# Last group of four tiles in an attention kernel: three of its six exponential additions move from POOL to VectorE

## What is computed

```python
def _L0_attn_ref(x, Wq, bq, Wk, bk, Wv, bv, Wo, bo):
    q = (x @ Wq + bq).reshape(B, S, H, DK)          # H = 16 heads, DK = 64
    k = x @ Wk + bk                                 # one key and one value for all heads
    v = x @ Wv + bv
    scores = jnp.einsum('bshd,btd->bhst', q, k) / np.sqrt(DK).astype(x.dtype)
    w = jax.nn.softmax(scores, axis=-1)
    out = jnp.einsum('bhst,btd->bshd', w, v).reshape(B, S, H * DV)
    return out @ Wo + bo

def _L0_ffn_ref(x, gate_w, gate_b, w1, b1, w2, b2, w3, b3):
    probs = jax.nn.softmax(logits, axis=1)          # over the tokens
    vals, idx = jax.lax.top_k(probs, 2)
    # three layers with relu for each of 8 experts, y; then
    v = jnp.einsum('ebso,bse->eo', y, w_tok)
    return jnp.einsum('bse,eo->bso', ind, v)

x = x + 0.5 * ffn(layernorm(x)); x = x + attn(layernorm(x)); x = x + 0.5 * ffn(layernorm(x))
```

## Time and profile before

| | us |
|---|---|
| median of 3 runs | 1040.29 |
| lowest and highest | 1039.52 and 1041.52 |
| the profiled execution, its device time | 1043.1 |
| its span, from the first to the last instruction | 1041.3 |

### The profile page before, as it was taken

The page is one execution under the profiler, slowest core; times in us unless marked ns, Lnnn a source line. Parts: engine busy times, 40 slices in busy tenths (PEclk is TensorE's granted clock), DMA queues, the critical chain, the costliest instruction groups (busy, mean ns, idle before and its releaser), DMA issues.

```text
span 1041.3 us, 18673 instructions
## 1 busy us (share of the span) xinstructions
PE 1008.1 (97%) x7140; PEld 660.8 (63%) x7140; DVE 767.7 (74%) x1029; ACT 619.1 (59%) x874; POOL 698.9 (67%) x367
## 2 busy tenths in 40 slices
PE   8899998899999999999999999999999998999996
PEld 6676886546657566556655665745565465876884
DVE  7989997867875676567576578556757646789996
ACT  5695565667754565456474467467746454685563
POOL 4475554766886689488498578756849757665653
PEclk9999998999999999999999999999999999999999
DMA  5720810001110100001001010012000213521612
GB/s 170 245 82 6 258 63 21 1 3 33 32 23 22 43 23 22 23 23 42 23 23 35 11 42 23 23 34 67 28 23 22 64 36 112 182 82 62 202 64 82
DMA packets 31407, 61.72 MB, mean 59 GB/s; under 512 B 10566, under 2 KB 15831, under 8 KB 31319
## 3 DMA queue, kind: packets, MB, share of 16 engines
q1 hardware_dynamic: 30096, 58.41, 18.7%
q10 hardware_dynamic: 1222, 2.12, 0.6%
HBM read 56.32 MB, written 3.67 MB: 58 GB/s over the span
## 4 chain that ended last, share of the span: by engine, by line
PE 84%; DVE 8%; issue 2%; ACT 2%; POOL 2%; DMA 1%; SPq 0%; DVEq 0%; ACTq 0%; POOLq 0%
PE ring L1047 21%; PE ring L981 6%; PE ring L1059 6%; PE ring L1005 5%; PE ring L1011 5%; PE ring L1007 5%; PE ring L1009 5%; PE ring L755 4%; PE ring L761 4%; PE ring L757 4%; PE ring L1020 3%; PE ring L778 2%; PE ring L779 2%; PE ring L781 2%; DVE ring L1606 2%
## 5 line engine op out<-in xcount | busy, mean ns | idle before, releaser
L1763 DVE TENSOR_REDUCE mx<-ring 128x2 f32<-128x1024 f32 x248 | 290.5, 1226 | 64.4 <-PE ring L981 64.3
L638 POOL TENSOR_TENSOR sum_picksT<-sum_picksT,P_wb 128x1024 f32<-128x1024 f32 x128 | 312.5, 2441 | 18.6 <-POOL sum_picksT L638 0.4
L1388 ACT ACTIVATE P_wb<-ring 128x1024 f32<-128x1024 f32 x256 | 262.3, 1027 | 54.6 <-PE ring L1011 25.2
L638 POOL TENSOR_TENSOR sum_picksT<-P_wb 128x1024 f32<-128x1024 f32 x64 | 166.5, 2601 | 166.4 <-ACT P_wb L1388 166.4
L696 POOL TENSOR_TENSOR R<-t,R 128x512 fp32r<-128x512 f32 x124 | 162.2, 1309 | 117.6 <-ACT R L1160 114.2
L1047 PE MATMUL ring<-P_wb,t 128*32 128x512 f32 x2048 | 228.4, 593 | 0.0
L1047 PEld LDWEIGHTS ring<-P_wb,t 128*32 128x32 f32 x2048 | 74.0, 110 | 138.6 <-issue 119.6
L1400 ACT COPY OZ<-ring 128x512 f32<-128x512 f32 x64 | 37.5, 586 | 156.3 <-PE ring L1047 147.5
L1160 ACT CAST R<-t 128x512 fp32r<-128x512 f32 x124 | 76.9, 620 | 74.6 <-PE ring L761 68.2
L981 PE MATMUL ring<-R 64*128 64x512 f32 x512 | 105.3, 407 | 1.0 <-ACT P_wb L1376 0.7
L1005 PE MATMUL ring<-R 64*128 64x512 f32 x512 | 102.5, 394 | 1.5 <-DVE MR L1768 1.5
(11 more groups left out here) (205 smaller groups left out, 1511.2 us busy)
## 6 DMA issues: line engine op xcount, KB each, us to landing
P_wb<-wd SPq DMA_DIRECT2D x64, 512.0 KB, 5.3
rzb<-rzd SPq DMA_DIRECT2D x64, 256.0 KB, 3.9
xs<-in_L_attn_x SPq DMA_DIRECT2D x8, 256.0 KB, 4.9
zrc<-SZ SPq DMA_DIRECT2D x128, 2.0 KB, 1.7
out<-xs SPq DMA_DIRECT2D x8, 256.0 KB, 2.8
sum_picksT<-in_L_ffn_w SPq DMA_DIRECT2D x2, 512.0 KB, 5.3
MR<-mT SPq DMA_DIRECT2D x62, 4.0 KB
t<-in_L_ffn_w SPq DMA_DIRECT2D x1, 512.0 KB, 6.4
```

The lines of the kernel that those rows point to most:

```text
L638: pool.tensor_tensor(US[:, g % 2, c, :, :], first, PU[:, TPB * c + t, :, :], ALU.add).then_inc(s_ua, 1)
L1388: act.activation(PU[:, u, :, :], ring[slot(("scores", g, u))][:, :, :], ACT.Exp, scale=SCALE).then_inc(s_exp, 1)
L1763: dve.tensor_reduce(mx[:, :, u] if g else mx0_unit[:, u // TPB, :, 0, u % TPB, 0], ring[slot(("max", g, u))][:, :, :], AX.X, ALU.max).then ...
```

## The change

For group 31 alone, POOL makes only the three additions of pair 0. The three of pair 1 are issued on VectorE, in a new function `add_last`, after the two subtractions of L1871 and ahead of moments(7). They count on a semaphore of their own, `s_last`. `sums(31)` waits for both semaphores, and SP's `first(4)` to `first(7)` wait for the new one. For a semaphore to be free, the reduction at the start of `update` counts on the existing `s_ln` in place of `v_chain`; it waits for itself as before.

```diff
@@ SP, late_weights
                 def first(e):
                     sp.wait_ge(s_pv, UNITS * (NQ - 1) + e + 1)
-                    sp.wait_ge(s_ua, (TPB - 1) * (PAIRS * (NQ - 1) + e // TPB) + max(e % TPB, 1))
+                    if e < TPB:
+                        sp.wait_ge(s_ua, (TPB - 1) * PAIRS * (NQ - 1) + max(e, 1))
+                    else:
+                        sp.wait_ge(s_last, max(e - TPB, 1))
                     load_wb(1, 0, e)
@@ POOL, attention
                 for g in range(NQ):
-                    for c in range(PAIRS):
+                    for c in range(PAIRS if g + 1 < NQ else 1):
                         add_exp(g, c)
@@ PE
             def sums(g, bank):
 
-                pe.wait_ge(s_ua, (TPB - 1) * PAIRS * (g + 1))
+                if g + 1 < NQ:
+                    pe.wait_ge(s_ua, (TPB - 1) * PAIRS * (g + 1))
+                else:
+                    pe.wait_ge(s_ua, (TPB - 1) * (PAIRS * g + 1))
+                    pe.wait_ge(s_last, TPB - 1)
@@ DVE
             def update(f):
                 s = F[f]
                 dve.wait_ge(s["l3_drained"], NU + 1)
-                dve.tensor_reduce(vv[:, :], vacc[:, :, :], AX.X, ALU.add).then_inc(s["v_chain"], 1)
-                dve.wait_ge(s["v_chain"], 1)
+                ln_link(dve.tensor_reduce(vv[:, :], vacc[:, :, :], AX.X, ALU.add))
...
+            def add_last():
+
+                g, c = NQ - 1, PAIRS - 1
+                dve.wait_ge(s_sf, g - 1)
+                for t in range(1, TPB):
+                    dve.wait_ge(s_exp, UNITS * g + TPB * c + t + 1)
+                    wait(dve, s_last, t - 1)
+                    first = PU[:, TPB * c, :, :] if t == 1 else US[:, g % 2, c, :, :]
+                    dve.tensor_tensor(US[:, g % 2, c, :, :], first, PU[:, TPB * c + t, :, :], ALU.add).then_inc(s_last, 1)
@@ DVE, attention, g == NQ - 1, behind the two subtractions
                             dve.tensor_tensor(xl[:, b2, :], back[b2], xh[:, b2, :].bitcast(F32),
                                               ALU.subtract).then_inc(F[1]["x_low"], 1)
+                        add_last()
```

More of the change, by code:

```diff
@@ L204, in ffn_sems @@
                      "ind_taken", "wsum_done", "wd_written", "l1_done", "l2_done", "l3_done", "relu2_done", "l3_drained",
-                     "h1_high", "h1_ready", "h2_high", "h2_ready", "h2_tail", "x_low", "x_high", "v_chain", "v_ready", "hv_ready",
+                     "h1_high", "h1_ready", "h2_high", "h2_ready", "h2_tail", "x_low", "x_high", "v_ready", "hv_ready",
                      "v_transposed", "VB_ready", "update_done", "x_updated")
@@ L219, in macaron_kernel @@
         s_st, s_exp = sem("scoresT_done"), sem("exp_done")
+        s_last = sem("last_exp_added")
         s_ua, s_sf, s_sz = sem("exp_added"), sem("sums_filled"), sem("sums_taken")
```

## The result

| | kernel before | changed kernel |
|---|---|---|
| median of 20 runs each, us | 1040.72 | 1038.01 |
| lowest to highest | 1038.06 to 1045.45 | 1036.05 to 1041.70 |
| span of the profiled execution | 1041.3 | 1038.6 |

The ratio is 0.9972, with a 95% interval of 0.9960 to 0.9984: 0.28% faster, 2.7 us by the medians. The measured gain is 0.6 us smaller, and over 20 runs the kernel before came out 0.4 us higher; together these are the 1.0 us between forecast and measurement.

The account below looks back on a forecast made before the run. TensorE, 97% busy, was taken as the bound, idling 2.86 us behind POOL's additions. That idle plus up to 2 us of lower clock, less about 1.3 of new waits, gave 3.3 at the low end: 1040.29 - 3.3 = 1037.0 us, range 1035.7 to 1039.2.

Parts of the forecast that it names:

- reduce(0) waits for P_wb: Sign that the whole is wrong: VectorE's reduce(0), forecast at 881.6 to 882.4 us, waits for the gate-weight DMA.
- POOL's additions set the sums, and the idle time goes: Ahead of sums(31): TensorE idles 2.86 us for POOL's last addition; after the change the sums start at about 872.75.
- An addition on VectorE at 1.23 us: Pair 1's three additions on VectorE: 1.23 us each, 3.8 us with gaps, ending at about 872.0.
- The upper bound, 3.02: Longest scale multiplication, taken as the most an addition on VectorE could cost: 9.1 us for three.
- The lower clock, up to 2 us: After the idle time TensorE runs at 1.2 GHz through layer2(0)'s first half; avoiding this gains up to 2 us.
- New waits of about 1.3 us ahead of layer2(0): TensorE waits for split(0), 0 to 0.5 us for the high part and about 0.8 for the low.
- The loads: Gate weights, issued by SP behind the slipped reciprocals(30), take 5.3 us and land at about 881.3, just before reduce(0).
- give part of it back: Rival, chance 0.10: loads or VectorE 1 us later before reduce(0), gain only 1.5 to 2.7 us, about 1038.2.
- The clock did not fall: Rival, chance 0.08: two short waits around 875 to 877 us lower TensorE's clock, 1.9 us lost, 1038.9.
- additions at 2.5 us: Rivals, 0.04 each: VectorE additions at 2.48 us give no visible change; beyond 2.45 it turns slower, 1042.2 at 3.02.
- The range: Forecast time 1035.7 to 1039.2 us, from 3.8 us gained plus over half the run spread, to the clock case.

Follow-up runs that it names:

- changed_again: The changed kernel unaltered, run and profiled a second time; ratio to the kernel before 0.9971 (0.9955 to 0.9986).
- spread: Changed kernel with both subtractions ahead of scale(29), moments(7) behind it, invert(7) and reciprocals(30) between the additions; 0.9971 and 0.9967 of the kernel before.
- changed_third: The changed kernel unaltered, run and profiled a third time; ratio to the kernel before 0.9979 (0.9960 to 0.9998).
- adds_doubled: Changed kernel with VectorE's first addition made four times, six additions in place of three; median 1042.82 us, ratio to the kernel before 1.0009.
- before_warm: Kernel before with 24 identity transposes on TensorE filling the idle time ahead of the sums of group 31; ratio 1.0007 (0.9990 to 1.0023).

## Why the prediction was right, and where its sum was not

The time lies in the range and the main mechanism is the predicted one, but that the number came so near is partly luck: two terms of the sum were too large and in part cancelled each other, the gain by the clock and the cost of the new waits. And one of the prediction's own signs of being wrong, that reduce(0) waits for P_wb, did come, in the first profile (1.32 us) and in changed_again (0.86).

- **POOL's additions set the sums, and the idle time goes.** Right: the sums start at 873.10, when layer1(0) ends, and the 2.6 to 2.9 us are gone in all three profiles.
- **An addition on VectorE at 1.23 us.** Right: 1.21 to 1.23, end at 872.27 against 872.0 worked out, in a profile that is 0.4 us late as a whole. The upper bound, 3.02, was that of a VectorE held up by POOL, and spread showed 2.59 for it.
- **The lower clock, up to 2 us.** About right in size where it happens (1.5 us for about 3.4 us at 0.50; the prediction had 1.9 for 3.8), wrong as a term of the sum: of three profiles of the kernel before one had it. This is the term that was most mis-sized.
- **New waits of about 1.3 us ahead of layer2(0).** Too high: 0.4 us were lost there. L1540 took 0.17 us with POOL idle, so split(0) started 0.3 us ahead of its range, counted from layer1(0); the wait for its low part was recorded as 0.24 us, the one for the high part not at all. This made up for about half of the clock.
- **The loads.** They were to land at 881.3 and landed at 883.0, 1.3 us late even when the 0.4 of the whole profile are taken off: first(0) was issued 3.59 us behind the reciprocals' end and not 2.97, since the write took 0.6 us more, and the load took 6.10 us in place of 5.3. That was the rival "give part of it back", whose mechanism came in the first profile and cost its full 1.3 us there, scale(30) included. In changed_third the loads came in time, in changed_again a shorter scale(30) made up for the wait.
- **Rivals.** The clock did not fall in any profile of the changed kernel; additions at 2.5 us would have made it slower or equal, as adds_doubled shows.
- **The range.** It took the kernel before to spread by 1 us on either side of its median, from three runs. Twenty ran from 1038.06 to 1045.45, with a median 0.4 us higher, so the range was narrower than its reasons allowed.

The ledger by the usual profiles: 2.6 to 2.8 us of idling removed, about 0.4 given back ahead of layer2(0), 2.3 to 2.4 left (152.1 to 149.75). The remaining 0.3 to 0.4 us to the 2.7 of the medians are within the interval, which is 1.2 us wide on either side, and need no cause. Executions of before in which the clock falls may be part of them, but before_warm, with a ratio of 1.0007, does not bear that out, and how often it falls was not measured. The 2.7 us between the two first profiles are a chance meeting of a costly execution of each kernel: the fall of the clock in one (1.7 us above the usual block), the late loads in the other (1.4 above).

## What to carry to other kernels

A chain on a slow engine that ends just ahead of the bounding one can be halved by giving its tail to an idle neighbour, if the neighbour starts when the slow one has let go of what they share; check what stands behind the new work on that engine, down to the DMAs that its results release. Whether a wait that a change puts on another engine has a price depends on the slack behind it and on what the delay does to the next operation there: 0.62 us were made up by a shorter scale(30) in one execution, and 1.08 made worse by a longer one in another. When an experiment takes work off an engine, look whether a wait has come in its place before reading the result. A cost that one profile shows (a fall of the clock, a late DMA) should be seen in a second one before it enters a sum.

## What the runs showed of the hardware

VectorE's operations that read two operands from SBUF are held up by POOL's additions and hold them up: 128x512 took 2.8 us beside POOL and 0.64 without, 128x1024 2.59 and 1.23, and POOL's addition 3.46 in place of 2.40. Which of them pays depends on who starts first: in the seven profiles in which scale(29) started ahead of POOL's second addition it took 1.23 to 1.33 us, in the six in which it started behind it (by 0.09 to 0.43 us) 3.04 to 3.38. The mean granted clock goes along with most of the spread between executions, as cause or as effect: in the kernel before, beside changed_again, nine runs at 0.996 had a mean of 1039.07 us, four at 0.989 of 1043.74; in changed_again three at 0.997 had 1036.93, five at 0.994 1038.61. At one place TensorE's clock stayed at 2.4 GHz behind idle times of 1.87, 2.59 and 2.78 us and fell to 1.2 GHz behind 2.86 and 3.46.
